# A depthwise 5x5 convolution by TensorE: four squares a channel in a bank alone, both parts of the taps in one product, and the splitting of the taps moved to VectorE

## What is computed

```python
# x: (128, 55, 55, 96) float32, kernel: (96, 5, 5) float32
k = jnp.transpose(kernel, (1, 2, 0))[:, :, None, :]
y = lax.conv_general_dilated(x, k, window_strides=(1, 1), padding='SAME',
        dimension_numbers=('NHWC', 'HWIO', 'NHWC'), feature_group_count=ch)
return x + y
```

## Time and profile before

| | us |
|---|---|
| median of 3 runs | 820.11 (819.94 to 821.16) |
| profiled execution | 820.36 |
| its span in the profile | 818.6 |
| PE busy | 811.2 (99%) |
| DVE busy | 538.9 (66%) |
| ACT busy | 617.4 (75%) |
| POOL busy | 620.6 (76%) |

### The profile page before, as it was taken

One profiled execution on the slowest core, in us unless ns is written; L12 is line 12 of the kernel. 1 busy time (PEld: TensorE's weight loads), 2 busy tenths in 40 slices (PEclk: granted clock), 3 DMA queues, 4 the chain that ended last, 5 costly groups with the idle time before them and its releaser, 6 DMA issues.

```text
span 818.6 us, 19694 instructions
## 1 busy us (share of the span) xinstructions
PE 811.2 (99%) x7217; PEld 809.2 (99%) x7217; DVE 538.9 (66%) x2224; ACT 617.4 (75%) x1157; POOL 620.6 (76%) x263
## 2 busy tenths in 40 slices
PE   8999999999999999999999999999999999999997
PEld 7999999999999999999999999999999999999997
DVE  6666666666666666666666666666666666666664
ACT  6777777777777777777777777777777777777774
POOL 2978878778696786977778878778696786977772
PEclk9999999999999999999999999999999999999999
DMA  9999999999999999999999999999999999999965
GB/s 370 418 414 393 388 387 386 392 385 396 395 389 393 375 402 388 387 391 383 395 391 391 389 386 386 395 381 395 395 387 394 380 399 381 390 390 391 389 246 232
DMA packets 32497, 313.40 MB, mean 383 GB/s; under 512 B 3600, under 2 KB 6800, under 8 KB 8080
## 3 DMA queue, kind: packets, MB, share of 16 engines
q1 hardware_dynamic: 31968, 311.67, 97.4%
q10 hardware_dynamic: 432, 0.46, 0.2%
HBM read 161.13 MB, written 150.99 MB: 381 GB/s over the span
## 4 chain that ended last, share of the span: by engine, by line
PE 98%; DMA 1%; DVE 0%; ACT 0%; ACTq 0%; issue 0%; DVEq 0%
PE sums L428 98%; DMA places_in<-places 1%; DVE x_low L254 0%; DVE weights L249 0%; DVE rest L235 0%; DVE taps_split L233 0%; DVE taps_split L237 0%; ACT y_out L323 0%; ACTq L219 0%; DVEq L163 0%; DVE y_out L357 0%; DVEq L228 0%
## 5 line engine op out<-in xcount | busy, mean ns | idle before, releaser
L428 PE MATMUL sums<-weights,x_high 121*128 121x226 f32 (+3 forms) x4800 | 804.1, 274 | 0.0
L428 PEld LDWEIGHTS sums<-weights,x_high 121*128 121x128 f32 x4800 | 729.0, 192 | 0.0
L428 PE MATMUL sums<-weights,x_low 121*128 121x226 f32 (+3 forms) x2400 | 659.1, 275 | 1.5 <-DVE x_low L254 1.5
L254 POOL TENSOR_TENSOR x_low<-x_in,x_high 121x1920 fp32r<-121x1920 f32 x95 | 411.9, 4336 | 175.3 <-ACT x_high L315 175.3
L323 ACT ACTIVATE y_out<-sums 128x264 f32<-128x264 f32 (+2 forms) x960 | 360.4, 398 | 189.8 <-PE sums L428 176.0
L428 PEld LDWEIGHTS sums<-weights,x_low 121*128 121x128 f32 x2400 | 460.8, 192 | 1.9 <-issue 1.9
L363 DVE TENSOR_TENSOR y_out<-sums,y_out 128x96 f32<-128x96 f32 (+3 forms) x1056 | 263.0, 249 | 123.3 <-ACT y_out L323 102.3
L315 ACT ACTIVATE x_high<-x_in 121x1920 fp32r<-121x1920 f32 (+1 forms) x195 | 295.2, 1514 | 5.3 <-DMA x_in<-x 5.2
L254 DVE TENSOR_TENSOR x_low<-x_in,x_high 121x1280 fp32r<-121x1280 f32 (+1 forms) x100 | 170.1, 1704 | 71.1 <-ACT x_high L315 71.1
L357 DVE TENSOR_TENSOR y_out<-sums,y_out 128x44 f32<-128x44 f32 (+2 forms) x768 | 152.0, 198 | 76.6 <-ACT y_out L323 76.3
L249 POOL TENSOR_TENSOR weights<-taps_split,places_in 121x450 fp32r<-121x450 f32 x95 | 133.7, 1407 | 7.2 <-DVE taps_split L237 7.2
(11 more groups left out here) (9 smaller groups left out, 1.9 us busy)
## 6 DMA issues: line engine op xcount, KB each, us to landing
x_in<-x SPq DMA_DIRECT2D x95, 1600.0 KB, 11.6
y<-y_out SPq DMA_DIRECT2D x95, 1536.0 KB, 7.5
taps_in<-taps SPq DMA_DIRECT2D x22, 150.0 KB, 11.8
x_in<-x SPq DMA_DIRECT2D x5, 320.0 KB, 5.3
y<-y_out SPq DMA_DIRECT2D x3, 302.5 KB, 2.5
y<-y_out SPq DMA_DIRECT2D x1, 357.5 KB, 3.7
taps_in<-taps ACTq DMA_DIRECT2D x2, 150.0 KB, 4.9
y<-y_out SPq DMA_DIRECT2D x1, 271.0 KB, 2.6
```

Source lines behind the costliest of these rows:

```text
L254: engine.tensor_tensor(x_low[slot][0:SQUARE, cols], x_in[c % X_SLOTS][0:SQUARE, cols], x_high[slot][0:SQUARE, cols].bitcast(F32), ALU.subt ...
L428: product = pe.matmul(sums, v[slot][0:SQUARE, at:at + IMAGES], window, start=n == 0 and v is x_low, stop=n == len(squares) - 1 and part == ...
```

## The change

1. `TILES` becomes 14 a channel: (0,), (1, 2), (3, 4) in strips 0 to 3, and (0, 1), (2, 3, 4) in strip 4. The four squares at the top of strips 0 to 3 have a bank alone (`alone`).
2. For such a square there are two products in place of three: `x_low` by the high part, and `x_high` by both parts of the taps at once, 2 x 182 = 364 columns in strip 0 and 2 x 196 = 392 in strips 1 to 3. The sums of the low part land beside the others in the same bank.
3. ACT copies all 14 tiles. DVE copies none, but adds the low sums of a square alone (L362), and, where there is a strip to the left, makes a second column seam from them (L376). The row seam (L367) waits for the DVE instruction before it.
4. The three steps of `split_taps` go from POOL to DVE, one a channel in the first three channels of each 4, between the low part of the next channel's piece 0 and the first tile.

```diff
 TILES = tuple((j, squares) for j in range(GRID) for squares in (
-    ((0, 1), (2, 3, 4)) if SUM_COLS[j][1] == EDGE else ((0, 1), (2, 3), (4,))))
+    ((0, 1), (2, 3, 4)) if j == GRID - 1 else ((0,), (1, 2), (3, 4))))
...
+def alone(tile):
+    return len(TILES[tile][1]) == 1
...
-                        if LATER_PIECES[piece][0] <= TILES[i][0] < end and copied_by_act(i):
+                        if LATER_PIECES[piece][0] <= TILES[i][0] < end:
                             copy_sums(c, i)
...
-                if copied_by_act(i):
-
-                    dve.wait_ge(tile_copied, copied(c, i))
-                else:
-                    dve.wait_ge(tile_copied, copied(c, i - 1))
-                    dve.wait_ge(tile_summed, summed(c, i))
-                    dve.tensor_copy(*fresh(c, i)).then_inc(y_step, 1)
+
+                dve.wait_ge(tile_copied, copied(c, i))
+                if alone(i):
+                    own, low_sums = fresh(c, i, LOW)
+                    dve.tensor_tensor(own, low_sums, own, ALU.add).then_inc(y_step, 1)
                 if row_seam(i):
+
+                    dve.wait_ge(y_step, stepped(c, i - 1))
...
+                    if alone(i):
+                        dve.wait_ge(y_step, stepped(c, i) - 1)
+                        dve.tensor_tensor(seam, sum_view(c, i, LOW)[:, :, 0:SEAM], seam, ALU.add).then_inc(y_step, 1)
...
                 if c < LAST:
                     split_low(dve, c + 1, 0, low_by_dve)
+
+                if c % BATCH < SPLIT_STEPS and c // BATCH + 1 < BATCHES:
+                    split_taps(dve, c // BATCH + 1, c % BATCH)
...
                 place_taps(pool, c)
                 split_low(pool, c, 1, low_by_pool)
-                if c % BATCH == BATCH // 2 and c // BATCH + 1 < BATCHES:
-                    split_taps(pool, c // BATCH + 1)
...
+                    if alone(i):
...
+                        pe.matmul(sums[:, HIGH], x_low[slot][0:SQUARE, at:at + IMAGES], windows[:, HIGH],
+                                  start=True, stop=False, skip_group_check=True)
+                        product = pe.matmul(sums, x_high[slot][0:SQUARE, at:at + IMAGES], windows,
+                                            start=False, stop=True, skip_group_check=True)
+                        break
```

More of the change, by code:

```diff
@@ L68, in end_row, with even @@
     return min(HEIGHT, SIDE * (square + 1) + HALO)
+def even(count):
+    return count + count % 2
 def tile_rows(tile):
@@ L73, in tile_rows @@
     return first_row(squares[0]), end_row(squares[-1])
-def copied_by_act(tile):
-    return len(TILES[tile][1]) > 1
+def alone(tile):
+    return len(TILES[tile][1]) == 1
 def row_seam(tile):
@@ L87, in col_seam @@
     return TILES[tile][0] > 0
-COPIES = [sum(copied_by_act(n) for n in range(i + 1)) for i in range(len(TILES))]
-STEPS = [sum((not copied_by_act(n)) + row_seam(n) + col_seam(n) for n in range(i + 1)) for i in range(len(TILES))]
+COPIES = [i + 1 for i in range(len(TILES))]
+STEPS = [sum(alone(n) + row_seam(n) + (1 + alone(n)) * col_seam(n) for n in range(i + 1)) for i in range(len(TILES))]
 COPIES_ALL, STEPS_ALL = COPIES[-1], STEPS[-1]
@@ L199, in y_view, with sum_view, fresh @@
             return y_out[c % Y_SLOTS][:, Y_AT[j]:Y_AT[j + 1]].rearrange("p (r c) -> p r c", c=FRESH[j])
-        def sum_view(c, i):
+        def sum_view(c, i, part=HIGH):
             first, end = tile_rows(i)
             cols = SUM_COLS[TILES[i][0]][1]
-            return psum[:, bank_of(c, i), 0:(end - first) * cols].rearrange("p (r c) -> p r c", c=cols)
-        def fresh(c, i):
+            at = part * even((end - first) * cols)
+            return psum[:, bank_of(c, i), at:at + (end - first) * cols].rearrange("p (r c) -> p r c", c=cols)
+        def fresh(c, i, part=HIGH):
             j = TILES[i][0]
@@ L210, in fresh @@
             new = first + SEAM if row_seam(i) else first
-            return y_view(c, j)[:, new:end], sum_view(c, i)[:, new - first:, FRESH_AT[j]:FRESH_AT[j] + FRESH[j]]
+            return y_view(c, j)[:, new:end], sum_view(c, i, part)[:, new - first:, FRESH_AT[j]:FRESH_AT[j] + FRESH[j]]
         def piece_cols(c, piece):
@@ L220, in load_taps, with split_taps @@
                              ).then_inc(taps_loaded[slot], 16)
-        def split_taps(engine, batch):
+        def split_taps(engine, batch, step):
             slot = batch % SPLIT_SLOTS
@@ L227, in split_taps @@
             centre = places_in[0:SQUARE, TAP_COLS:].unsqueeze(1).broadcast_to([SQUARE, BATCH, TURNED_COLS])
[L228 to L237, removed]
+            if step == 0:
+                engine.wait_ge(taps_loaded[batch % TAPS_SLOTS], 16 * (uses(batch, TAPS_SLOTS) + 1))
+                if batch >= SPLIT_SLOTS:
+                    c = (batch - SPLIT_SLOTS + 1) * BATCH - 1
+                    engine.wait_ge(weights_ready[c % SLOTS], uses(c, SLOTS) + 1)
+                engine.tensor_tensor(high, given, centre, ALU.add).then_inc(taps_step, 1)
+            elif step == 1:
+                engine.wait_ge(taps_step, SPLIT_STEPS * batch + 1)
+                engine.tensor_tensor(left, high.bitcast(F32), centre, ALU.subtract).then_inc(taps_step, 1)
+            else:
+                engine.wait_ge(taps_step, SPLIT_STEPS * batch + 2)
+                engine.tensor_tensor(low, given, left, ALU.subtract).then_inc(taps_step, 1)
         def place_taps(engine, c):
@@ L344, in finish_sums @@
                 first, end = tile_rows(i)
-                if not (row_seam(i) or col_seam(i)):
+                if not (row_seam(i) or col_seam(i) or alone(i)):
                     return
                 y, sums = y_view(c, j), sum_view(c, i)
-                if copied_by_act(i):
-                    dve.wait_ge(tile_copied, copied(c, i))
-                else:
-                    dve.wait_ge(tile_copied, copied(c, i - 1))
-                    dve.wait_ge(tile_summed, summed(c, i))
-                    dve.tensor_copy(*fresh(c, i)).then_inc(y_step, 1)
+                dve.wait_ge(tile_copied, copied(c, i))
+                if alone(i):
+                    own, low_sums = fresh(c, i, LOW)
+                    dve.tensor_tensor(own, low_sums, own, ALU.add).then_inc(y_step, 1)
                 if row_seam(i):
+                    dve.wait_ge(y_step, stepped(c, i - 1))
                     seam = y[:, first:first + SEAM]
@@ L372, in _ @@
             dve.wait_ge(places_loaded, 16)
-            split_taps(dve, 0)
+            for step in range(SPLIT_STEPS):
+                split_taps(dve, 0, step)
             place_taps(dve, 0)
@@ L399, in wait_bank @@
                     return
-                if row_seam(before) or col_seam(before):
+                if row_seam(before) or col_seam(before) or alone(before):
                     pe.wait_ge(y_step, stepped(c + back, before))
@@ L419, in tile @@
                     run = lead + count + (lead + count) % 2
+                    if alone(i):
+                        if cols == WINDOW:
+                            windows = weights[slot][0:SQUARE, :, origin:origin + run]
+                            sums = psum[:, bank_of(c, i), 0:2 * run].rearrange("p (w n) -> p w n", w=2)
+                        else:
+                            windows = weights[slot][0:SQUARE, :, origin:origin + (end - first) * WINDOW].rearrange(
+                                "p w (r c) -> p w r c", c=WINDOW)[:, :, :, first_col:first_col + cols]
+                            sums = psum[:, bank_of(c, i), 0:2 * run].rearrange("p (w r c) -> p w r c", w=2, c=cols)
+                        pe.matmul(sums[:, HIGH], x_low[slot][0:SQUARE, at:at + IMAGES], windows[:, HIGH],
[3 more added lines that the diff above has]
+                        break
                     for v, part in ((x_low, HIGH), (x_high, HIGH), (x_high, LOW)):
```

## The result

| | us |
|---|---|
| changed kernel, median of 4 runs | 834.12 (833.84 to 834.29) |
| kernel before, median of 4 runs beside it | 820.63 (819.94 to 821.72) |
| ratio | 1.0166 (95% interval 1.0151 to 1.018) |
| span of the profiled execution | 832.2 (818.6 before) |

What follows compares the result with a forecast made beforehand. PE, 99% busy, was taken as bound by weight loads; afterwards DVE's late add would stall it. 95 channels at 8.50 for 8.378 add 11.6, ends take 0.2 and 0.6: 818.6 + 10.8 = 829.4, plus 1.8: 831 us, range 802 to 838.

Steps and rivals of the forecast that it cites:

- The sum: Whole kernel: 95 channels at 8.50 us in place of 8.378, small savings at the end, 831 in all; chance 70%.
- What is saved on PE: On PE, four fewer weight loads a channel make a channel without stalls 8.16 us, 0.22 less than before.
- The pair of a square alone: On PE, the two products of such a square take 0.28 us from start to next tile.
- Placing of the taps: On POOL, it takes 1.04 us, starting 1.70 and 1.02 after a channel's start in turn.
- p + p': Lengths of a channel and the one before it, together 17.00 us, so a mean of 8.50.
- The holding and what it delays: POOL's placing holds DVE's `x_low`, so tile 0's add ends late and PE waits 0.68 us at tile 8 in long channels.
- The start after a wait: On PE, tile 8 starts 0.14 us after the add that frees its bank, bounds 0.06 to 0.20.
- DVE's other work: 27 seams, adds and copies a channel in place of 22, 6.39 us; engine full, but costed at nothing.
- Rival 1: DVE goes ahead of POOL, `x_low` runs clear and only the product saving is left: 799 us (797 to 803), 12%.
- a floor at 8.38 a channel: Within the 12% case of DVE ahead of POOL, DMA could bind, stuck at 8.38 us a channel: 808 us.

Runs made afterwards that it cites:

- the last run: Changed kernel with POOL's placing waiting for DVE's low part from the third channel, five row seam waits gone, wide products without their high half: 782.56 us.

## Why the prediction was right, point by point

- **The sum.** 831 was forecast, 834.12 measured, in a range of 802 to 838 and in the forecast's own, 823 to 837. The mean channel is 8.514 for 8.50; a short one and the long one behind it together are 17.03 (8.26 + 8.77) for 17.00. Of the 3 us missing, 1.8 are the first channel: 10.28 in the profiled execution, where the sum has 8.50 as for the others. It is the same path with another term: DVE's `x_low` of the second channel starts 4.05 after the first channel's start, waiting for ACT, and not 1.80, so tile 8 goes at 6.22 (15.92 - 9.70). In the kernel before, tile 8 wanted nothing from DVE's list, and the first channel took 8.48.
- **What is saved on PE** was mis-sized by a little: 8.213 for 8.16. The wide product is 0.182, at the upper bound (0.181) that the 226-column products had given, and above the proportion from the 512-column ones, 0.172, that I took. It makes 95 x 0.05 = 5 us of the product saving, and next to nothing of the forecast: a later tile 8 (4.25 for 4.19) shortens PE's wait by what the products cost more. The pair of a square alone, forecast at 0.28, is 0.31 from its start to the next tile, and the product behind it follows 0.01 sooner than usual. The Trainium skill's N / 2.4 + 2.5 ns (TensorE: Matmul & The Clock Gate, section Back-to-back issue gap) would be 0.166, for a product alone; in a stream with weight loads it measured 0.016 more. The 131 ns that it gives there for 512 columns in a stream with weight loads is out, since 392 columns took more.
- **Placing of the taps.** Forecast at 1.70 and 1.02 in turn after a channel's start, measured 1.67 and 1.06 at 351.79 and 360.61. Its end, 2.72 behind a channel of 8.21, is 10.93 after the start of the channel before, for 10.90: these 0.03 are most of what p + p' is off by.
- **The holding and what it delays.** `x_low` was to be about 2.3 and 1.5 to 1.6 long: 2.27 and 1.59. The gap was to be ahead of tile 8 alone, released by L362: so it is.
- **The start after a wait** was taken as 0.14, from the start of the program. In mid-stream it is 0.06 to the first product (356.48 to 356.54), and 0.10 that the second product loses, since the loads had stood too: 0.16 in all. So the term was right in size and wrong in its parts. The second part also touches the short channels, which were to have no wait. At 360.61 the add ends at 4.14 and tile 8 goes on time, but the product behind it comes 0.05 late, and the channel is 8.26 for 8.21.
- **DVE's other work.** "I cost it at nothing" held for the time (fewer waits, no gain). In the short channels `x_low` started 1.93 after the channel's start (362.54 - 360.61), not 1.85, but POOL holds it to 2.17 there, so it cost nothing either.
- **Rival 1's remark**, that a POOL that waits would take its turn ahead of the splitting step and stall PE in three channels of four, was shown by turning the order round. There most channels are 8.9 to 9.1 in three of four, and 8.21 in the fourth.
- **DMA** gave no sign of a floor at 8.38 a channel: 8.213 ran for 94 channels on end, and 7.93 to 7.96 in the last run.

## What to carry to other kernels

Ask of every instruction that a change gives to an engine what already stands ahead of it in that engine's list, and who waits for its end: here a new add of 0.33 us turned a saving on PE into a loss of 1.7%, because it stood behind 2.7 us of work for later channels (2.27 and 0.38), and swapping it with one neighbour gave back 14.7 us. Two engines that were seen to hold one another should be ordered by a wait rather than left to meet, and in the right order: a wait of POOL on DVE turned the loss into a gain of 1.4%, and the reverse order cost 5.4%. And an engine that never pauses is a suspect, not a verdict: take work from it at one place and see whether the time moves.

## What the runs showed of the hardware

- A product is a weight load as long as its columns take less: 0.1117 us for 182 to 226 columns with operands of the narrower type (fp32r), and 0.182 for 364 to 392 (four of them take 0.283 beyond their loads).
- A product that had waited for a bank started 0.06 us after the add that freed it, and the next came 0.21 behind it in place of 0.11, the loads having stood as well. A wait costs PE 0.10 beyond its own gap.
- DVE with both operands in SBUF and POOL reading SBUF exclude one another for whole instructions: the earlier goes on and the later stands (`x_low` 2.27 for 1.49, POOL's placing 2.01 for 1.04). When DVE's instruction ended, the waiting one of POOL went ahead of DVE's next: a step of 0.47 on DVE lasted 1.32. DVE's adds with one operand in PSUM stayed at 0.33.
- PE's granted clock was at 0.50 for 3.4 us, once 6.8, in the first channel in eight of the nine profiles of the changed kernel and its variants, and in neither profile of the kernel before. It cost 1.6 us where it fell behind tile 8 (35 products in 5.7 us in place of 4.1), and next to nothing in the changed kernel itself, where PE had to wait for the add anyway.
- This one is of the kernel rather than of the chip: channels can alternate. A long channel brings the placing earlier within the next, which makes that one short. The sum of two is what stays (17.03), and the median channel, 8.50, looks like none of them.
